# Moving 23 of 98 index scatters in between the edge gathers of a graph attention layer, and one inverse root from the 84th scatter to the 81st

## What is computed

```python
h = relu(layernorm(x))
# attention: every node has a loop to itself besides the 12,500 edges
alpha = sum(xs_j * a_s) + sum(xd_i * a_d)           # 8 heads
a = softmax of leaky_relu(alpha) over the edges of one target, times the edge weight
out = segment_sum(xs_j * a) + bias
h1 = layernorm(out + h) * g1 + b1
x + layernorm(h1 + gelu(h1 @ W1.T + b1) @ W2.T + b2) * g2 + b2
```

## Time and profile before

| what | value |
|---|---|
| median of 3 runs | 3205.0 us (3204.89 to 3207.64) |
| the profiled execution's own time | 3220.57 us |
| its span | 3218.7 us |
| PE, DVE, ACT, POOL busy | 93%, 70%, 56%, 54% of the span |
| mean granted clock of PE | 0.976 of full speed |

### The profile page before, as it was taken

The page is one execution under the profiler, slowest core; times in us unless marked ns, Lnnn a source line. Parts: engine busy times, 40 slices in busy tenths (PEclk is TensorE's granted clock), DMA queues, the critical chain, the costliest instruction groups (busy, mean ns, idle before and its releaser), DMA issues.

```text
span 3218.7 us, 56922 instructions
## 1 busy us (share of the span) xinstructions
PE 2983.5 (93%) x19965; PEld 2702.6 (84%) x19965; DVE 2242.2 (70%) x6228; ACT 1803.1 (56%) x3373; POOL 1725.5 (54%) x1494
## 2 busy tenths in 40 slices
PE   4887246999999999999999999999999999999998
PEld 4776235999999998999999999899999999899997
DVE  6887544777777777777777777777777777777775
ACT  4776243555555555555555555555555555555554
POOL 5765464555555555555555555555555555555552
PEclk9999577999999999999999999999999999999999
DMA  5446564222222222222222222222222222222210
GB/s 154 146 144 134 104 168 103 51 57 57 59 59 57 60 60 60 60 60 60 60 60 60 60 60 60 58 53 57 57 58 58 59 59 60 60 60 60 60 47 27
DMA packets 86976, 228.72 MB, mean 71 GB/s; under 512 B 19353, under 2 KB 23487, under 8 KB 86692
## 3 DMA queue, kind: packets, MB, share of 16 engines
q1 hardware_dynamic: 53803, 145.86, 13.7%
q0 software_dynamic: 31664, 78.07, 12.8%
q10 hardware_dynamic: 1225, 1.15, 0.1%
HBM read 146.85 MB, written 78.20 MB: 70 GB/s over the span
## 4 chain that ended last, share of the span: by engine, by line
PE 79%; DVE 2%; ACT 1%; issue 1%; POOL 1%; DMA 0%; DVEq 0%; POOLq 0%; ACTq 0%
PE ps_f L1342 33%; PE ps_a L1357 11%; PE ps_a L1359 11%; PE ps_a L1358 11%; PE ps_x L1379 8%; PE ps_t L1389 3%; PE ps_t L1367 2%; DVE act_lo L1207 1%; DVE arena L1147 0%; ACT h L728 0%; ACT ps_f L754 0%; DVE n_stat L908 0%; POOL n_rstd L599 0%; ACT arena L767 0%; ACT act_hi L753 0%
## 5 line engine op out<-in xcount | busy, mean ns | idle before, releaser
L1207 DVE TENSOR_TENSOR act_lo<-ps_f,act_hi 128x512 fp32r<-128x512 f32 x784 | 539.1, 688 | 732.1 <-ACT ps_f L754 731.4
L753 ACT ACTIVATE act_hi<-ps_f,hidden_bias 128x512 fp32r<-128x512 f32 x784 | 537.2, 685 | 849.1 <-PE ps_f L1342 849.1
L1357 PE MATMUL ps_a<-ffn_hi,act_hi 128*128 128x256 f32 x3136 | 892.0, 284 | 3.3 <-DVE arena L1173 3.3
L1359 PE MATMUL ps_a<-ffn_hi,act_lo 128*128 128x256 f32 x3136 | 876.6, 280 | 0.0
L1358 PE MATMUL ps_a<-ffn_lo,act_hi 128*128 128x256 f32 x3136 | 875.0, 279 | 0.0
L1342 PE MATMUL ps_f<-zt_hi,ffn_hi 128*128 128x512 f32 x1568 | 623.7, 398 | 3.3 <-DVE zt_lo L1165 1.6
L1357 PEld LDWEIGHTS ps_a<-ffn_hi,act_hi 128*128 128x128 f32 x3136 | 588.0, 187 | 41.5 <-issue 5.6
L1342 PE MATMUL ps_f<-zt_hi,ffn_lo 128*128 128x512 f32 x1568 | 619.8, 395 | 0.0
L1342 PE MATMUL ps_f<-zt_lo,ffn_hi 128*128 128x512 f32 x1568 | 619.6, 395 | 0.0
L1358 PEld LDWEIGHTS ps_a<-ffn_lo,act_hi 128*128 128x128 f32 x3136 | 589.2, 188 | 27.7
L1359 PEld LDWEIGHTS ps_a<-ffn_hi,act_lo 128*128 128x128 f32 x3136 | 588.8, 188 | 0.0
(11 more groups left out here) (230 smaller groups left out, 5345.4 us busy)
## 6 DMA issues: line engine op xcount, KB each, us to landing
xb<-in_x SPq DMA_DIRECT2D x98, 512.0 KB, 6.0
out<-arena SPq DMA_DIRECT2D x98, 512.0 KB, 5.2
msgs<-arena SPq DMA_DIRECT2D x49, 256.0 KB, 2.5
arena<-msgs SPq DMA_DIRECT2D x49, 256.0 KB, 7.1
sums<-arena SPq DMA_DIRECT2D x49, 256.0 KB, 5.4
arena<-sums,node_rows POOLq DMA_INDIRECT x392, 3.8
xb<-in_x,arena POOLq DMA_INDIRECT x196, 2.8
arena<-in_w_t SPq DMA_DIRECT2D x2, 1024.0 KB, 7.5
```

The costliest lines, as they stand in the source:

```text
L753: act.activation(act_hi[:, m % AB, :], ps_f[:, m % 2, :], ACT.Gelu, bias=hidden_bias[:, m:m + 1]).then_inc(act_hi_ready, 1)
L1207: dve.tensor_tensor(act_lo[:, m % AB, :], ps_f[:, m % 2, :], act_hi[:, m % AB, :].bitcast(F32), ALU.subtract).then_inc(act_lo_ready, 1)
L1357: pe.matmul(to, act_hi[:, m % AB, cols], ffn2[0][:, m, :], start=(m == 0 and t % 2 == 0), stop=False, skip_group_check=True)
L1359: ins = pe.matmul(to, act_lo[:, m % AB, cols], ffn2[0][:, m, :], start=False, stop=(m == MF - 1), skip_group_check=True)
```

## The change

A new tuple `PLACE_AT` = 4, 6, ..., 48 names 23 pairs of stage 1. Behind the four gathers of each of them POOL now issues one scatter. Its two waits for `target_ready` and `rows_cleared` move with the first, to pair 4. The remaining 75 scatters follow behind the last gather, as before. The three inverse roots stand ahead of scatter 31, 41 and 81 instead of 8, 20 and 84.

```diff
-RSTD_AT = (8, 20, 84)
+PLACE_AT = range(4, 49, 2)
+RSTD_AT = (len(PLACE_AT) + 8, len(PLACE_AT) + 18, len(PLACE_AT) + 58)
...
             def pair(j):
                 gather(j)
+                if j.n == PLACE_AT[0]:
+                    pool.wait_ge(target_ready, 1)
+                    pool.wait_ge(rows_cleared, 16 * RB)
+                if j.n in PLACE_AT:
+                    place(Step(0, PLACE_AT.index(j.n), NCH))
             pool.wait_ge(in_order, 1)
             steps(pool, pair, 0, NPAIR, *PAIR_LOOP)
-            pool.wait_ge(target_ready, 1)
-            pool.wait_ge(rows_cleared, 16 * RB)
-            steps(pool, place, 0, NCH, NCH, NCH, RB)
+            steps(pool, place, len(PLACE_AT), NCH, NCH, NCH, RB)
```

More of the change, by code:

```diff
@@ L130, in build @@
     EMPTY = EP
-    assert D == KC * P and NT % TG == 0 and NCH % 2 == 0 and NCH < P and EP % BLOCKS == 0 and NPAIR > RELU2_AT and NCH > RSTD_AT[2] and D == 2 * P
+    assert D == KC * P and NT % TG == 0 and NCH % 2 == 0 and NCH < P and EP % BLOCKS == 0 and NPAIR > max(RELU2_AT, PLACE_AT[-1]) and NCH > RSTD_AT[2] and D == 2 * P
     sums = nc.dram_tensor("sums", (EP + P, D), F32, kind="Internal").ap()
```

## The result

The changed kernel takes 3167.93 us (median of 4, 3162.05 to 3169.01) against 3204.94 us for the kernel before: ratio 0.988, 95% interval 0.9863 to 0.9897, so 37 us faster, where 28 were forecast.

What follows compares the result with a forecast made beforehand. PE paces the nodes, but POOL's scatter list and then the sum pairs set their start; -29.0 + 2 - 1.5 - 1 = -29.5 us, taken as -28 for the slow profile: 3177 us, range 3167 to 3193.

Steps and rivals of the forecast that it cites:

- The third root: Before node group 2: root behind 59 tail scatters, done some 11 us ahead of need, removes ACT's whole wait, -29.0 us.
- The DMA beside the later sum pairs and PE's slow start: Sum pairs 27 on: transfers once hidden in the wait cost +2 us; PE's slow start behind it disappears, -1.5 us.
- The edge pairs: Gather loop of stage 1: 23 added scatters make POOL pace the pairs, lengthening the loop 3 us, bounds 0 to 8.
- the packets themselves are nothing: Edge pairs: the moved scatters' packets load the DMA engines negligibly, 0.02 us of each engine per scatter.
- gather landings stay near 3 us: Edge pairs, expected sign in the profile after: gathers sharing POOL's queue with scatters land about as before.
- the tightest pair: Edge pair 17: its last gather lands 3.7 us before DVE reads it, the slack against a later POOL.
- landings past 6 us: Edge pairs, sign that the prediction is wrong: gathers taking more than 6 us to land.
- slower: gathers wait for the landing of the scatter: Rival, edge pairs: delays beyond 3.7 us paid in 11 rounds, +20 us at the median landing; chance 0.05.
- The second root and the softmax: Edge pairs' end to softmax: root behind 19 tail scatters instead of 20, -4.7 and +3.5, together -1 us (-5 to +5).
- The end of the scatters: Before the fix-up: POOL ends scatters near 456, loads tables near 462, hidden by some 15 us; no cost.
- more than forecast: Rival: fewer scatters beside sum pairs, second root at -5, no added DMA work; -36 us or more, 3165 to 3169; chance 0.05.

Runs made afterwards that it cites:

- e14: Kernel before with only the third inverse root moved, behind scatter 59 instead of 84, on a chip like that of the result; ratio 0.9943 to before.
- e15: Kernel before, all scatters still behind the gathers, roots behind scatters 4, 9 and 59, on a chip like that of the result; ratio 0.998 to before.
- e16: Changed kernel with 12 scatters between gathers (every fourth pair), roots behind scatters 16, 20 and 60, on a chip like the result's; ratio 0.9893 to before.
- e13: The changed kernel once more, unaltered, on a chip like that of the result; ratio 0.9876 to the kernel before.
- e5: The changed kernel, unaltered, on a chip with late edge pairs; ratio 1.003 to the kernel before.
- e11: Kernel before plus a plain 128 x 4 byte store on POOL's queue at the 23 places, on a chip with late edge pairs; ratio 0.9991 to before.
- e3: Changed kernel with roots at 30, 42 and 84, so the scatters moved alone, on a chip with late edge pairs; ratio 1.009 to before.
- e18: Same edit as e3, run again on a chip with late edge pairs; ratio 1.0099 to the kernel before.
- e4: Kernel before plus a small unused POOL power operation at the 23 places, no transfers, on a chip with late edge pairs; 3270.97 us, single execution.

## Why the prediction was right, and where it was wrong

**The third root: right.** -29.0 forecast, -29.1 in the traces. Its margin was larger than worked out (finished 17.7 us ahead of need, not 11), since the 40 scatters between the second and the third root took 58.0 us (336.2 to 394.2), 1.45 us each, where 1.86 was taken from the earlier trace rows.

**The DMA beside the later sum pairs and PE's slow start: about right.** +2 and -1.5 forecast, -1.3 measured together. But the 41.2 us are not the floor: in e14, e15 and e16, where POOL's tables come after the sums, the same pairs took 34.7, 35.6 and 33.6. In the changed kernel they fall into them, as before. Timelines of POOL, DVE and PE there:

```profile
431.01 0.59 POOL L618 DMA_DIRECT2D node_rows<-row_of  x1 [8.08 <-DMA row_of<-arena]
433.25 2.36 POOL L645 TENSOR_TENSOR arena<-xb,rows 128x1024 f32<-128x1024 f32 x1
...
431.25 0.69 DVE L1126 TENSOR_TENSOR arena<-ps_a,rows 128x512 f32<-128x512 f32 x1 [2.10 <-DMA sums<-arena]
433.05 3.11 DVE L1119 TENSOR_TENSOR arena<-arena 128x512 f32<-128x512 f32 x1
436.68 0.68 DVE L1119 TENSOR_TENSOR arena<-arena 128x512 f32<-128x512 f32 x1
...
429.25 1.10 PE L1329 MATMUL ps_a<-arena 128*128 128x256 f32 x4 [0.70 <-DVE arena L1119]
430.19 0.38 PE L1318 MATMUL ps_f<-ident,arena 128*128 128x128 f32 x2
432.64 2.05 PE L1329 MATMUL ps_a<-arena 128*128 128x256 f32 x4 [2.07 <-DVE arena L1119]
436.26 2.04 PE L1329 MATMUL ps_a<-arena 128*128 128x256 f32 x4 [1.15 <-issue]
```

DVE waits 2.10 us for a store, then one of its weighings takes 3.11 us instead of 0.68 while POOL adds 128 x 1024 elements, and PE's four matmuls take 2.05 us instead of 1.10 for the next pairs (granted clock 0.53 from 432 to 443 us). The one long weighing stands beside the one such addition in the kernel before too (2.40 us) and in e13 (3.22); in e14 to e16, where the addition comes after the sums, none is over 1 us. The Trainium skill (SBUF — State Buffer, "SBUF: two separate sides") says that a DVE operation with two inputs in SBUF and a GpSimd operation that reads SBUF lock each other out of a shared port. The 3.11 us agree: about the 2.36 of the addition and the usual 0.68. By the same place of the Trainium skill the one that starts first keeps the port, while in this trace DVE's record begins 0.20 us ahead of POOL's and DVE is the one that waits.

**The edge pairs: right in size on the chip of the result, wrong elsewhere, and the mechanism was half of it.** +3 (0 to 8) forecast, +4.65 measured. POOL does become what paces the pairs: from pair 11 on no gather waits more than 0.4 us for ACT, where waits of 1 to 2.3 us stood up to pair 48 before, and DVE waits now and then. But "the packets themselves are nothing" and "gather landings stay near 3 us" were wrong: behind a scatter they are 4.3 to 5.6 us at the median, and this takes the greater part of the 3.7 us that the tightest pair had to spare. The prediction costed the packets by their own share of the engines and took from the start in order that landings do not matter; it named landings past 6 us as a sign of being wrong, and some reached 7.1. So the rival "slower: gathers wait for the landing of the scatter" came near: the delay of 1.5 to 2.6 us at the median stayed under its 3.7, and by the rival's sum anything beyond 1 to 2 us more would have been paid in every round. That the +3 came close with this left out is in part luck. (By its own numbers POOL would be 5.6 us late, not 5.4, which changes nothing.) How the 4.65 divides between POOL's time and the landings no run on such a chip tells. On the other chips the same scatters cost 48 us in some other way (e5, e11).

**The second root and the softmax: the step that failed.** "Together -1 us, between -5 and +5" was mis-sized: -15.9 in the traces, and -6.6 against e14 (349.9 to 343.3), where the surplus of the first profile is out of it. The step took the pace between the root and the gathers' end from one execution (3.5 us a scatter between the 5th and the 20th, with landings up to 17.3 us) and held it fixed. Before, 20 scatters took 63.5 us from the end of the gathers to the root, and 54 in e14; in the changed kernel 19 took 38, though they began 9 us later. What could be gained here was more than the bound of -5: e14 has 42.5 us from the edge pairs to the scan, of which 30.8 remain where the root is not waited for (e15, e16), so nearly 12, less what the edge pairs lose. The DMA was freer when the burst began, first in e14, then in the changed kernel (columns as above):

```profile
295.00:305.00 10.00, 8.25 (x61) 7.34 (x61) 6.10 (x20) 7.60 (x19) 0.97 (x1) 1.00 0.96 94
...
295.00:305.00 10.00, 8.34 (x64) 7.67 (x63) 8.11 (x29) 6.67 (x18) 7.25 (x8) 1.00 0.69 177
```

In e14 the engines are full at 94 GB/s, with four scatters out, and POOL issues one thing in ten us; in the changed kernel it issues eight. (In e14 POOL waits 4.00 us there for a scatter to land.) That the last gathers, still being made then, keep the scatters from piling up beside SP's bulk loads is how I read it; no run separates it. With the 2.9 us of the first sum pairs, for which no term stood, this makes the difference: 28 + 5.6 + 2.9 is 36.5 us, and 38.7 with what the last rows of the table add; 37 and 39 were measured (the result and e13).

**The end of the scatters: the effect was right, the reason too small.** The tables were forecast at 462, hidden by 15 us, and came at 431, hidden by 24 us before the last record. What the prediction did not say is that this keeps the gain of the third root from being lost: without the interleaving the tables come at 472, and the fix-up waits 11 us for them (e14). The two parts of the change are not a main part and a cost; each needs the other's bound gone. e3 and e18 add that with the scatters moved the root's place had no wait left to remove. That was not tried on a chip like that of the result; in the changed kernel's trace scatter 84 (counted from zero) goes out at 400.43, 13 us ahead of ACT's need at 413.64.

**The range** reached to 3167 and the median was 3167.93, at its very edge. The case that occurred is the rival "more than forecast" (36 us or more), which had a chance of 0.05. Of its reasons the softmax at -5 or better held and the first sum pairs had fewer scatters beside them; that no DMA work was added did not. By the terms and bounds of the prediction itself the range would run from 3168 (the softmax at -5 is 4 us better than -1, not 5) to 3191, not from 3167 to 3193.

**Left open:** why the first profile of the kernel before was slower in the softmax; why chips differ by 80 us in the edge pairs, and why an indirect scatter costs up to 2 us there while a plain store of the same size costs none; why a gather lands later behind a scatter; why the scatters of e15 go slower than those of e14.

## What to carry to other kernels

When a wait hides the length of another engine's list, the wait's removal is worth only the slack of that list: look at what that engine still has to issue, and when its last result is read. Work can be moved out of a congested list into a stretch where the engine waits anyway, but in doses: 12, 23 and 45 scatters gave different answers, and for 23 the sign depended on the chip. A median of landings is no proof that nothing is delayed: look at which transfers it counts, and at those right behind the moved ones. And a pace taken from one profiled execution that stands 15 us above its median belongs in the bounds, not in the sum.

## What the runs showed of the hardware

- The same program took 3205 us on two occasions and 3275 to 3285 us on three other chips, the difference being mostly in the edge pairs, where ACT had waits of up to 5.7 us on such a chip (e5) and of at most 2.5 us on the chip of the result.
- Scatters of 128 x 4 bytes between gathers of 128 x 1024 bytes raised the DMA share from 0.47 to 0.66 at the same 143 GB/s. The first gather behind a scatter landed after some 5.6 us for 3.0, the last of its pair after 4.3 for 2.8 (changed kernel and before). Plain stores of 128 x 4 bytes raised the share as well (0.64 in e11 for 0.38 in e4).
- On the chips with late edge pairs a scatter between gathers cost 0.7 to 2.1 us, a plain store of the same bytes nothing, and POOL's time alone nothing.
- Beside one POOL addition of 2.36 us a DVE product of 0.68 us took 3.11 us, 3.22 in e13 and 2.40 in the kernel before.
